# FFN branch q: rows sorted by leaf group between its two linears, and k's second linear ahead of it

## What is computed

```python
# per branch f in q, k, v; x is the normed input, 384 x 1024
leaf = hard binary tree of depth 4 over x @ node_w.T     # 16 leaves
hidden = relu(x @ w1[leaf] + b1[leaf])                   # 64 wide, the token's own leaf alone
out_f = hidden @ w2[leaf] + b2[leaf]                     # 1024 wide
# then
x = x + softmax(out_q @ out_k.T / 32) @ out_v
```

## Time and profile before

| | |
|---|---|
| median of 3 runs | 727.94 us (725.6 to 729.39) |
| profiled execution | 726.86 us, its span 725.1 us |
| TensorE busy | 702.6 us, 97% of the span |
| VectorE, ScalarE, GpSimd busy | 476.5, 402.0, 229.2 us |
| granted TensorE clock, mean | 0.997 |
| bytes moved | 105.15 MB, mean 145 GB/s |

### The profile page before, as it was taken

One profiled execution on the slowest core, in us unless ns is written; L12 is line 12 of the kernel. 1 busy time (PEld: TensorE's weight loads), 2 busy tenths in 40 slices (PEclk: granted clock), 3 DMA queues, 4 the chain that ended last, 5 costly groups with the idle time before them and its releaser, 6 DMA issues.

```text
span 725.1 us, 11736 instructions
## 1 busy us (share of the span) xinstructions
PE 702.6 (97%) x4490; PEld 669.4 (92%) x4490; DVE 476.5 (66%) x957; ACT 402.0 (55%) x692; POOL 229.2 (32%) x203
## 2 busy tenths in 40 slices
PE   3999999999999999999999999999999998999987
PEld 3989999998999999999999999998899998889886
DVE  6758774874777477766666565656766466787543
ACT  5455556464565565768686775422523457677340
POOL 4634332232332332227022274470004511422120
PEclk9999999999999999999999999999999999999998
DMA  5421635413313223231313152234135749896242
GB/s 212 160 107 59 231 138 211 176 60 120 109 67 117 73 102 117 90 118 58 117 59 117 59 209 73 109 121 138 41 136 193 272 164 378 307 413 220 117 145 88
DMA packets 21766, 105.15 MB, mean 145 GB/s; under 512 B 5696, under 2 KB 6080, under 8 KB 12912
## 3 DMA queue, kind: packets, MB, share of 16 engines
q1 hardware_dynamic: 12880, 80.84, 30.4%
q0 software_dynamic: 8544, 23.41, 8.9%
q10 hardware_dynamic: 288, 0.14, 0.1%
HBM read 92.71 MB, written 18.06 MB: 153 GB/s over the span
## 4 chain that ended last, share of the span: by engine, by line
PE 87%; DVE 6%; ACT 3%; DMA 2%; issue 1%; DVEq 0%; ACTq 0%
PE g_bank L1772 37%; PE g_bank L1797 12%; PE o_bank L1847 4%; PE t_bank L1836 4%; PE s_bank L2150 2%; PE s_bank L1824 2%; PE s_bank L1825 2%; PE g_bank L1726 2%; PE s_bank L2398 2%; PE s_bank L2360 2%; PE s_bank L2358 2%; PE s_bank L2359 2%; PE t_bank L2150 2%; DVE w_lo L1138 1%; PE g_bank L2332 1%; PE t_bank L2251 1%
## 5 line engine op out<-in xcount | busy, mean ns | idle before, releaser
L1772 PE MATMUL g_bank<-act_hi,w_hi 128*128 128x384 f32 x488 | 170.0, 348 | 0.0
L1772 PE MATMUL g_bank<-act_hi,w_lo 128*128 128x384 f32 x488 | 163.7, 335 | 0.0
L1772 PE MATMUL g_bank<-act_lo,w_hi 128*128 128x384 f32 x488 | 163.4, 335 | 0.0
L1138 DVE TENSOR_TENSOR w_lo<-raw,w_hi 128x2048 fp32r<-128x2048 f32 x58 | 137.3, 2367 | 36.0 <-ACT w_hi L675 34.0
L675 ACT ACTIVATE w_hi<-raw 128x2048 fp32r<-128x2048 f32 x67 | 128.1, 1912 | 30.3 <-PE s_bank L2150 12.5
L490 POOL DMA_INDIRECT edge_table<-ew,eidx x51 | 68.2, 1336 | 164.3 <-DMA edge_table<-ew,eidx 158.0
L1772 PEld LDWEIGHTS g_bank<-act_hi,w_hi 128*128 128x128 f32 x488 | 91.8, 188 | 2.7 <-issue 2.6
L1772 PEld LDWEIGHTS g_bank<-act_lo,w_hi 128*128 128x128 f32 x488 | 91.9, 188 | 0.0
L1772 PEld LDWEIGHTS g_bank<-act_hi,w_lo 128*128 128x128 f32 x488 | 91.6, 188 | 0.0
L437 POOL TENSOR_TENSOR w_lo<-raw,w_hi 128x2048 fp32r<-128x2048 f32 x10 | 47.0, 4695 | 103.5 <-ACT w_hi L675 97.2
L1275 DVE TENSOR_TENSOR pT_lo<-t_bank,pT_hi 128x384 fp32r<-128x384 f32 x96 | 50.6, 554 | 33.6 <-ACT pT_hi L768 33.2
(11 more groups left out here) (324 smaller groups left out, 1643.5 us busy)
## 6 DMA issues: line engine op xcount, KB each, us to landing
raw<-wstream_dram SPq DMA_DIRECT2D x68, 1024.0 KB, 4.8
xg<-xs POOLq DMA_DIRECT2D x12, 512.0 KB, 7.9
ys<-y_ring POOLq DMA_DIRECT2D x12, 512.0 KB, 4.6
x_sb<-x_dram SPq DMA_DIRECT2D x3, 512.0 KB, 5.0
y_acc<-x_dram POOLq DMA_DIRECT2D x3, 512.0 KB, 5.7
out_dram<-out_sb SPq DMA_DIRECT2D x6, 256.0 KB, 2.0
edge_table<-ew,eidx POOLq DMA_INDIRECT x51, 2.5
edge_table<-mask POOLq DMA_DIRECT2D x1, 576.0 KB, 3.5
```

What stands on the lines that cost most here:

```text
L1138: V.tensor_tensor(flat(w_lo[to][:, :, :]), raws[raw_slot(n.base)], flat(w_hi[to][:, :, :]), ALU.subtract) \
L1772: last = mm(out, w2[a], x2[b], start=k == 0 and a + b == 0, stop=not after and k == KT - 1 and a == 1)
```

## The change

Branch q keeps its dense first linear, but its second is done sorted, as k's and v's are:

- q's first: the four units' masked hidden values are merged by VectorE with a running maximum into `hc` (two tiles of 128x384): only the token's own group is above zero. TensorE turns `hc` to rows (`q_hidden_rows`, 6 transposes, in k's first pair), ScalarE copies them, GpSimd scatters them by q's `row_of` to `hs` in HBM and loads the sorted tiles back to `hq_win`. `hidden_T` for q reads `hq_win`, one a pair in k's second.
- Stage order: q first, k first, k second, q second, v first, v second. `U_STAGE` gives the units, `U_FIRST` those of k and v, `U_SECOND` those of k, q and v.
- The sort starts earlier: `count` stands at (u, m, k) = (1, 0, 3) and not (1, 1, 1), `route` right behind unit 0's two tiles, ahead of the split of unit `U_FFN + 2`. Sorted tiles 0 and 1 of k are transposed in unit 3 of q's first. On GpSimd k's rows go first, `load_pair(0)` waits for them alone, and the selections of q and v are scattered later, v's rows later still.
- k's rows come back in q's second: `bring_k` gathers them into `xg`, and `pair_T` and `take_tile` treat them as three more tiles (tiles 8 to 10 of 15) that go to `kf`. q's rows come back as k's did, by `back_T` in v's second.
- (`BACK` is `PAIRS + 2`.) The four `raw` buffers are used from `U_FFN + 2` on (before: from `U_SORT + 2`), the four `w4` slots from `U_SORT` on. ScalarE and VectorE swap the halves of y. The first copy of y waits for v's row scatters (`rows_out`).

```diff
-U_SORT = U_FFN + 2 * GROUPS
-U_DEEP = U_SORT + 2
+U_SORT = U_FFN + GROUPS
+U_DEEP = U_FFN + 2
+U_STAGE = [U_SORT + GROUPS * s for s in range(5)]
+U_FIRST, U_SECOND = [U_STAGE[0], U_STAGE[3]], [U_STAGE[1], U_STAGE[2], U_STAGE[4]]
+BRANCH = (1, 0, 2)
...
+def tile_of_pair(i):
+    return i if i < BACK else i + NT
...
                 if U_DEEP + 2 <= n < U_DEEP + 4:
-                    sp.wait_ge(g_full, OUT_FILL0)
+                    sp.wait_ge(sel_ready, 1)
...
+            sort_rows(1)
+            sort_sel(1)
+            pool.wait_ge(rows_out, 16 * NT)
+            load_pair(0)
+            pool.wait_ge(sel_out, 16 * NT)
+            load_sel(1)
+            bias_rows(1)
+            for i in range(1, 4):
+                load_pair(i)
+            sort_sel(0)
+            sort_sel(2)
+            load_pair(4)
+            load_pair(5)
+            pool.wait_ge(hn_ready, 2)
+            for t in range(NT):
+                nc.gpsimd.indirect_dma_start(hs, rows_of(0, t), hq_win[:, t, :], None,
+                                             bounds_check=ROWS - 1, oob_is_err=False).then_inc(hn_out, 16)
+            pool.wait_ge(hn_out, 16 * NT)
+            pool.dma_start(hq_win[:, :, :], hs.rearrange("(s p) m -> p s m", p=P)).then_inc(hw_in, 16)
+            pool.wait_ge(sel_out, 16 * 3 * NT)
             load_sel(0)
+            load_sel(2)
+            sort_rows(2)
             bias_rows(2)
+            pool.wait_ge(rows_out, 16 * 2 * NT)
+            load_pair(6)
+            load_pair(7)
+            for i in range(PAIRS):
+                store_pair(i)
+                if i == 3:
                     bias_rows(3)
+            store_pair(PAIRS)
+            stored(0)
+            for t in range(NT):
+                bring_k(t)
+            for i in range(PAIRS + 1, 2 * PAIRS):
+                store_pair(i)
+                if i == PAIRS + 1:
+                    load_pair(8)
                     mask_b1(3)
+                if i == PAIRS + 3:
+                    bias_rows(4)
+                if i > PAIRS + 2:
+                    load_pair(i - PAIRS + 6)
+            bring_back(1)
...
             def take_y(i):
+                if i == 0:
+                    act.wait_ge(rows_out, 16 * 2 * NT)
...
+            first_linear(0)
+            route()
+            split_lo(Index(U_FFN + 2))
+            first_linear(1)
+            leaf_bias(0, b1_st, top, low16)
+            split_lo(Index(U_FFN + 3))
...
+                    if (u, m, k) == (3, 0, 6):
+                        taken(fill_of(Index(U_FFN + 1)))
+                        pair_T(0)
+                    if (u, m, k) == (3, 1, 1):
+                        sel_T(0)
+                    if (u, m, k) == (3, 1, 4):
+                        pair_T(1)
+                    if (u, m, k) == (3, 1, 6):
+                        sel_T(1)
...
+            def hidden_T(i):
+                f, p = divmod(i, PAIRS)
+                if f == 1:
+                    pe.wait_ge(hw_in, 16)
+                    src = hq_win[:, p, :]
                 else:
+                    pe.wait_ge(h_ready, PAIRS * (f // 2) + p + 1)
+                    src = h_nat[:, p % 2, :]
+                o_taken(("h", i))
...
+                for b in ((0, 1), (2,))[f]:
+                    for p in range(PAIRS):
+                        def in_pair(half):
+                            if (p, half) == (0, 0):
+                                hidden_T(PAIRS * (b + 1) - 1)
+                            if (b, p, half) == (0, 0, 1):
+                                sel_T(2)
+                                sel_T(3)
+                            if b == 0 and half == 0 and p:
+                                hidden_T(PAIRS + p - 1)
+                            if b == 1 and half == 1 and p in (0, 2):
+                                pair_T(PAIRS + p // 2)
+                            if b == 1 and half == 1 and p >= NT:
+                                pair_T(BACK + p - NT)
+                            if b == 1 and half == 0 and p in (1, 2):
+                                sel_T(3 + p)
+                            if b == 2 and half == 0:
+                                back_T(p)
+                        second_pair(b, p, in_pair)
```

More of the change, by code:

```diff
@@ L2255, in _ @@
-            for u in range(GROUPS):
-                n = Index(U_SECOND[0] + u)
-                def bias_T(m, out):
-                    if (u, m) == (0, 0):
-                        pe.wait_ge(b_ready, 1)
-                        pe.wait_ge(selT_ready, 2)
-                    return mm(out, b2_st[:, u * MB + m * P:u * MB + (m + 1) * P], selT[:, 0:N], start=False, stop=True)
-                def in_second(m, k):
-                    if u >= 2 and (m, k) == (0, 4):
-                        pair_T(u - 2)
-                gemm_T(n, h_hi, h_lo, after=bias_T, at_end=lambda: taken(fill_of(n)), between=in_second)
+                    if (u, m, k) == (3, 0, 6):
+                        taken(fill_of(Index(U_FFN + 1)))
+                        pair_T(0)
@@ L2300, in hidden_T, with q_hidden_rows @@
                 for c in range(2):
-                    last = nc.tensor.transpose(o_bank[:, c * P:(c + 1) * P], h_nat[:, i % 2, c * P:(c + 1) * P], ident[:, :])
+                    last = nc.tensor.transpose(o_bank[:, c * P:(c + 1) * P], src[:, c * P:(c + 1) * P], ident[:, :])
                 last.then_inc(hT_full, 1)
+            def q_hidden_rows():
+                for c in range(2):
+                    if c == 0:
+                        taken(Index(OUT_FILL0))
+                    for t in ((0, 1), (2,))[c]:
+                        for m in range(2):
+                            at = (t - 2 * c) * MB + m * P
+                            last = nc.tensor.transpose(s_bank[c][:, at:at + P], hc[:, m, t * P:(t + 1) * P], ident[:, :])
+                    last.then_inc(hn_full, 1)
@@ L2361, in second_pair @@
                     if j == 0:
[L2362 to L2363 removed]
+                        pe.wait_ge(b_ready, (2, 3, 5)[b])
+                    mm(out, selT[rows, p * P:(p + 1) * P], b2_st[rows, half * 512:(half + 1) * 512],
                        start=False, stop=True).then_inc(y_full, 1)
@@ L2471 @@
     first = {f: units(arr(f"L0_ffn_{f}_w1").transpose(1, 0, 2).reshape(D, D)) for f in "qkv"}
-    second = {f: (units if f == "q" else leaf_rows)(arr(f"L0_ffn_{f}_w2").reshape(D, D)) for f in "qkv"}
+    second = {f: leaf_rows(arr(f"L0_ffn_{f}_w2").reshape(D, D)) for f in "qkv"}
     mix = {0: mk[0], U_Q0: mq[0]}
@@ L2482 @@
     stream += list(units(arr("L0_mix_Wout"))) + list(halves(gnn["wo"].T))
-    for f in "qkv":
-        stream += list(first[f]) + list(second[f])
+    for w in (first["q"], first["k"], second["k"], second["q"], first["v"], second["v"]):
+        stream += list(w)
     wstream = np.stack(stream)
```

576 lines of the change are left out of this document (297 added, 279 removed).

## The result

The changed kernel takes 737.92 us (median of 3 runs, 737.39 to 740.87) against 727.94: a ratio of 1.0151, interval 1.0125 to 1.0177. It is slower by 10 us where I forecast 7.4 us faster. The profiled execution took 737.39 us.

A forecast was written before the change was run, and what follows sets the result against it. TensorE, busy 702.6 of 725.1 us, was taken as the bound. Net 13.8 us less work gave 713.1; waits of 4.5 and 1.5 and 1 for full queues made 720.1, stated as 720.5, range 713 to 728.

The forecast's parts named there:

- A pair is 14 matmuls of 128x512, 0.23 us each: Price of q's second as six sorted pairs, taken from k's second: 19.9 us for six.
- The work removed: TensorE work gone: q's dense second, 36.4 us, and late weights in k's first, 4.2; together 40.6 us.
- The indices: Earlier sort in q's first: row indices ready at 539.8, 9.4 us earlier; six scatters issued until 550.6.
- The front: End of q's first: TensorE late for k's tiles 0 and 1 by 2 to 6 us, taken as 3.
- The first copy of y: k's second: waits for v's scattered rows, TensorE passes at 596.6; delay 4.5 us in all, the front's 3 included.
- k's gather: q's second: k's rows return at 623 to 634, wanted at 628; wait taken as 1.5 us, bounds 0 and 6.
- My sign of being wrong: TensorE's waits between 553 and 640 under 3 or over 12 us, or VectorE's weight splits holding k's second.
- The tail: Stretch behind the last y: unchanged at 34 us.
- The slower one: Rival: GpSimd's serial scatter, wait, load chain with 11.6 us landings, perhaps a lower TensorE clock; 731.7 us; chance 0.10.
- Transfers that pace the middle: Rival: k's first to q's second limited to 357 GB/s, 27.5 MB taking 77.0 us; 723.9 to 727; chance 0.17.
- all is hidden: Rival: scatters land in under 5 us, so no wait shows; 713 to 716.5 us; chance 0.20.
- my sum of TensorE work: Time with no new wait: 40.6 us goes, 26.8 comes, net 13.8 less than 726.86, giving 713.1 us.

The follow-up runs named there:

- full rows: Edit of the changed kernel: its 48 bias matmuls read all 128 rows again, not 64; alone 728.69 us, ratio 1.0035.
- v's early scatters: Changed kernel with 128-row bias matmuls, plus only v's row scatters issued ahead of the wait for q's hidden: 725.08 us, ratio 0.9969.
- run 3: Changed kernel with 128-row bias matmuls and new GpSimd order (v's scatters earlier; bias mask and one store before k's gathers): 723.53 us, ratio 0.9951.
- run 5: Changed kernel with the new GpSimd queue order alone, bias matmuls left on 64 rows: 738.69 us, ratio 1.0137.
- run 1: Kernel before the change, with only the bias matmuls of k and v cut to 64 rows: 739.51 us against 727.51, ratio 1.0168.
- run 11: Repeat of run 3's kernel (128-row bias matmuls, whole new GpSimd order): 724.02 us, ratio 0.9947.
- run 8: Run 3's kernel with k's three tiles for q's second loaded from x, not gathered; k's values wrong: 724.31 us, ratio 0.997.
- run 9: Run 3's kernel with all sorted tiles of k and v, k's returning tiles and selections loaded from x; output wrong: 723.17 us, ratio 0.9935.
- run 2: Changed kernel with its bias matmuls back on 128 rows, GpSimd's order as in the changed kernel: 728.69 us, ratio 1.0035.
- run 7: Run 3's kernel with k's first four tiles loaded from x ahead of the scatters; k's values wrong: 725.3 us, ratio 0.9967.
- run 4: Run 3's kernel with SP's weight loads held until k's scattered rows have landed: 723.54 us, ratio 0.9954.
- run 6: Run 3's kernel with tile 1's load right behind tile 0's and two bias operations later: 727.15 us, ratio 0.9998.

## Why the prediction was wrong

By the ratios, in us of 727.94, the changed kernel is at +11.0, full rows bring it to +2.5, v's early scatters to -2.3, the store queue to -3.9 (run 3: -3.6), and the forecast was -7.4. So of the 18.4 us by which I was out, 8.4 are the rows of the bias matmul, 4.8 a wait behind v's scatter, 1.6 the store queue (inside the noise) and 3.6 the rest. This holds for the edits in this order: with the queue changed first it gives nothing (run 5), and the rows then give 14.7 to 15.2.

- **The step that failed**: "A pair is 14 matmuls of 128x512, 0.23 us each". 12 of a pair's 14 are; the two bias matmuls cost 0.36 more each, and that of a first pair 0.38 (run 1). 36 and 12 of these are 17.5 us. In the kernel before, 24 and 12 of them make 13.2, of which 12.0 show in the time; in after, taking them away gives 9.2 us with the old queue and 14.7 to 15.2 with the new one (738.7 to 724.0 and 723.5); the rest does not show in the time. k's and v's linears, which I carried over unchanged, became dearer as well, 24 of the 36 halves being theirs. No row of before shows a 64-row matmul; I should have bounded it as an operation unseen.
- **The work removed** was right in the main: q's dense second is gone, and so are the late weights of k's first. But these were never 4.2 us. TensorE stood idle for 2.3 of the 26.4 us, and I compared with 22.2 for v's first, which took 23.2 from its first matmul. The same misplaced cut made k's second 21.9 in place of 21.2, so that 1.0 too much goes and 0.7 too much comes, and the sum is hardly off by it. With full rows k's first took 24.1 us, TensorE busy 23.9 of it.
- **The indices**: predicted 539.8 and a first scatter at 540.6; it began at 539.31, in a trace that runs 1.1 us ahead of that of before. Right. The six scatters took 10.3 us, one of them 2.37 at the start: right.
- **The front**: I took 3 us for TensorE's delay, and 6.9 for the landing. The rows took 10.3 from the last scatter's start (9.3 from its end), the load 3.8. TensorE waited 2.3, its granted clock then read 0.60 from 557 to 560, and the eight transposes took 1.94 us, 1.09 being their time behind a wait at full clock (run 11). q's first ended at 567.2, 4.4 us behind my floor of 563.9 less the 1.1. I had named the clock in a rival and given it nothing in the forecast.
- **The first copy of y**: mechanism right, TensorE's transpose of q's first tile to pass at 596.6. It passed at 600.6, so 5 us later on the shifted clock, but TensorE lost only 0.7 there, since its slow halves had delayed it by as much. On full rows this wait shows, 2.2 us in k's second. I had put the scattered rows' landing at 5.2 to 6.9 from the end of the last scatter; it took 8.8 (9.8 from its start).
- **k's gather**: 1.5 us with bounds 0 and 6: 0 in after, 1.7 to 2.6 on full rows. Right in size; but a plain load in its place was as late (run 8), so it was not the gather that made the wait.
- **My sign of being wrong** said nothing: TensorE's waits between 553 and 640 add up to 3.3 us in after, inside the 3 to 12 that I allowed, and none of my signs looked at what a matmul costs.
- **The tail**: 34.3 us, as said.
- **The rivals.** The slower one, GpSimd's chain with 11.6 us landings, is not why it was slower. By its own measure, from the end of the last scatter, its three landings took 9.3, 5.2 and 8.8 us. Transfers that pace the middle: in run 11, k's first to q's second moved at 303, 362 and 380 GB/s, so 357 is no limit over a stage; but landings grow where the queues are full: while the load of 8.24 us was under way in run 9, 421 and then 413 GB/s were moved. That all is hidden is not had even in run 9.

**What stays open.** The stages at their best in runs 2, 9 and 11 (29.4, 24.1, 21.8, 26.7 less its wait of 2.0, 23.5, 22.7, 34.2), put behind 534.7, make a span of 715.1 and a time of 716.9. That is 3.8 over my sum of TensorE work, and 4.6 where one counts the 0.8 us by which run 9's trace is ahead of that of before. Of these 4.6, 1.0 is q's first (564.1 for 563.1), 1.9 k's first (24.1 for 22.2), 1.3 v's first (23.5 for 22.2) and 0.4 the rest; 1.0 each in k's and v's first is the misplaced cut. What the remainder is made of stays open. And no run had all of these at once: whether a better order of GpSimd's queue could reach it, or whether transfers as a whole forbid it, these runs do not tell.

## What to carry to other kernels

Read a diff for shapes as carefully as for order: an operand's partitions, halved to fit two selections in one buffer, cost more than the whole restructuring won (9.2 us and more, against 3.6 to 3.9 that are left to win on full rows). If a matmul's form in the new code is in no row of the old trace, it is unpriced, however small it looks, and its count must be multiplied out over all the loops that share the helper. And where waits on several transfers are within 2 us of each other, price the second and third as well as the first: removing one gives what lies between them, and a slowdown elsewhere can hide them all until it is mended.

## What the runs showed of the hardware

- **A 64-row weight load beside 128-row matmuls is not overlapped.** Ahead of it the loader idles 0.36 us, behind it 0.24; a 128-row load among 128-row matmuls has no idle at all. The form saves nothing in return: its matmul takes 493 ns from start to modelled end, the 128-row form 392. The Trainium skill (TensorE: Matmul & The Clock Gate, "Step-by-step: what each phase is for") has the loads pulled ahead when row groups do not conflict or the load goes to the background buffer, and counts the row count as without effect on the load's time. The traces agree that the load's own time hardly moves (183 against 188 ns), and show that its place in time does. The Trainium skill (same page, "The mechanism") also says that a load overlaps only where the row group differs; the 128-row loads under 128-row matmuls here contradict that.
- **A wait of 2 to 4 us can halve the clock behind it.** Behind the 2.3 us wait eight transposes took 1.94 us, behind the 3.0 us wait 1.97; the granted clock was 0.50, the lower of its two levels (1.2 GHz), from 558 to 561 of after, from 630.5 to 633 of run 9, and from 563 to 566 of run 7, behind its 3.6 us wait. Not every wait did it: behind 1.7 us in run 2 and 2.0 in run 11 the clock stayed at 1.00, and the eight transposes took 1.09. Some 3 us at half speed are 1.5 us of work lost, an estimate, on top of the wait.
- **Landings depend on what runs beside them.** Half a MB from x or `xs` landed in 3.8 (after), 6.97 (run 4) and 8.24 us (run 9), a selection in 3.33 (run 7) and 7.38 (run 6). k's scattered rows landed 10.3 us from the start of the last scatter in after, and within 6.4 with the weight loads held back (run 4).
